# Preparing a group's pair products earlier, merging a tile later, and gathering rows three groups ahead

## The reference

```python
x = x0
for k in (k0, k1, k2):
    x = jnp.einsum('bhd,bmd,ohm->bod', x, x0, k)
    outputs.append(jnp.sum(x, axis=-1))
z = jnp.concatenate(outputs, axis=1)
h = jnp.maximum(jnp.concatenate([z, dense_ctx], axis=1) @ W_top1 + b_top1, 0.0)
h = jnp.maximum(h @ W_top2 + b_top2, 0.0)
y = h @ W_top3
```

## Time and profile before

| | us |
|---|---|
| median of 3 runs | 705.52 |
| the profiled execution | 703.25 |
| its span, first to last instruction | 701.4 |
| first chunk of stretch 0 | 42.91 |
| first chunk of stretch 15 | 615.18 |
| last chunk's end | 645.58 |

### The profile page before, as it was taken

One profiled execution on the slowest core, in us unless ns is written; L12 is line 12 of the kernel. 1 busy time (PEld: TensorE's weight loads), 2 busy tenths in 40 slices (PEclk: granted clock), 3 DMA queues, 4 the chain that ended last, 5 costly groups with the idle time before them and its releaser, 6 DMA issues.

```text
span 701.4 us, 12405 instructions
## 1 busy us (share of the span) xinstructions
PE 648.2 (92%) x2558; PEld 470.5 (67%) x2558; DVE 592.3 (84%) x1346; ACT 520.7 (74%) x1753; POOL 495.3 (71%) x443
## 2 busy tenths in 40 slices
PE   0289989899999999899999999999989999999998
PEld 0156767677676777676766767677767677777583
DVE  1649898898979898989889898989898989978890
ACT  0438877687777877777777878787777877889693
POOL 6636878687868788788878797978878884665000
PEclk9999999999999999999999999999999999999999
DMA  6362120303021211203130312121120313010100
GB/s 212 96 226 76 26 99 12 101 18 98 28 81 45 79 46 48 76 10 111 14 102 17 93 31 79 46 79 46 34 90 11 104 22 100 14 50 0 31 0 1
DMA packets 56674, 43.04 MB, mean 61 GB/s; under 512 B 37007, under 2 KB 40335, under 8 KB 56352
## 3 DMA queue, kind: packets, MB, share of 16 engines
q1 hardware_dynamic: 51488, 41.08, 19.3%
q0 software_dynamic: 5120, 1.32, 1.9%
HBM read 40.41 MB, written 1.97 MB: 60 GB/s over the span
## 4 chain that ended last, share of the span: by engine, by line
PE 45%; issue 14%; POOL 13%; DVE 13%; DMA 9%; SPq 4%; ACT 1%; DVEq 1%; POOLq 0%; ACTq 0%
PE Y L621 10%; PE Y L623 10%; PE Y L622 10%; DVE parts L535 7%; POOL x0g L320 6%; POOL parts L361 6%; PE X L588 5%; DVE pairs L475 4%; DMA pairs<-scratch 4%; SPq L275 3%; PE GB L595 2%; DMA scratch<-x0g 2%; DMA x0g<-in_table,rows_now 2%; PE X L653 1%; PE X L651 1%
## 5 line engine op out<-in xcount | busy, mean ns | idle before, releaser
L430 ACT ACTIVATE scaled<-Y,xtok 128x128 f32<-128x128 f32 x1280 | 353.4, 396 | 62.6 <-PE Y L623 60.0
L621 PE MATMUL Y<-k1lo,x1hi 128*128 128x512 f32 x640 | 294.6, 460 | 16.9 <-DVE parts L535 15.4
L623 PE MATMUL Y<-k1hi,x1lo 128*128 128x512 f32 x640 | 253.2, 396 | 0.0
L622 PE MATMUL Y<-k1hi,x1hi 128*128 128x512 f32 x640 | 252.4, 394 | 0.0
L535 DVE SCALAR_TENSOR_TENSOR parts<-Y,xtok,parts 128x128 f32<-128x128 f32 x768 | 213.1, 340 | 18.0 <-PE Y L623 17.4
L361 POOL TENSOR_TENSOR parts<-parts,scaled 128x512 f32<-128x512 f32 x128 | 185.8, 1452 | 30.2 <-ACT scaled L430 19.2
L320 POOL DMA_INDIRECT x0g<-in_table,rows_now x160 | 170.5, 1066 | 42.2 <-issue 37.5
L621 PEld LDWEIGHTS Y<-k1lo,x1hi 128*128 128x128 f32 x640 | 120.2, 188 | 74.9 <-DVE parts L535 31.9
L622 PEld LDWEIGHTS Y<-k1hi,x1hi 128*128 128x128 f32 x640 | 120.6, 188 | 40.7 <-issue 14.4
L623 PEld LDWEIGHTS Y<-k1hi,x1lo 128*128 128x128 f32 x640 | 120.2, 188 | 29.1
L475 DVE TENSOR_TENSOR pairs<-pairs,A 120x512 f32<-120x512 f32 x112 | 120.9, 1080 | 21.5 <-DMA pairs<-scratch 21.4
(11 more groups left out here) (74 smaller groups left out, 391.1 us busy)
## 6 DMA issues: line engine op xcount, KB each, us to landing
pairs<-scratch SPq DMA_DIRECT2D x112, 240.0 KB
A<-scratch SPq DMA_DIRECT2D x16, 240.0 KB
k1raw<-in_k SPq DMA_DIRECT2D x1, 2560.0 KB, 11.5
x0g<-in_table,rows_now POOLq DMA_INDIRECT x160, 2.4
k2s<-in_k SPq DMA_DIRECT2D x1, 2560.0 KB, 9.1
scratch<-x0g SPq DMA_DIRECT2D x96, 20.0 KB, 1.7
pairs<-in_w SPq DMA_DIRECT2D x3, 256.0 KB, 2.9
w2s<-in_w SPq DMA_DIRECT2D x1, 512.0 KB, 3.9
```

Of the source, the lines that this page charges most:

```text
L430: ins = nc.scalar.activation(block_of(to, i), Y[(NCH * tile + c) % YB][:, i * O:(i + 1) * O], ACT.Copy, scale=xtok[slot % 2][:, j, m:m + 1])
L621: nc.tensor.matmul(y, hi[:, tok], k1lo[:, cols], start=True, stop=False)
L622: nc.tensor.matmul(y, hi[:, tok], k1hi[:, cols], start=False, stop=False)
L623: nc.tensor.matmul(y, lo[:, tok], k1hi[:, cols], start=False, stop=True).then_inc(s_y, 1)
```

## The change

The places come from a table instead of a formula: products move to places 0, 2, 12, 20, 22, 29, 30, and the first-layer products to 12, 14, 22, 24, 26, 32, 34. A tile's merge stands behind chunk 5 of the next tile instead of chunk 2, `make_G` behind chunk 9 instead of 8. GpSimd gathers three groups ahead, 3, 2, 3 and 2 gathers in the four tiles. With two buffers for gathered rows, a gather then waits for the stores of the group that is one ahead (`s_scratch`), where it waited for products. The third group's rows are gathered before the loop.

```diff
-XTOK_AT, PROD_AT, PROD_APART, L0_LAG = 14, 6, 3.6, 6
...
-GATHER_TILES = 3
-MERGE_AT = 2
-G_AT = 8
...
+STEPS = {
+    "prod0": 0, "ph0": 1, "prod1": 2, "ph1": 4, "pl0": 9, "pl1": 10, "prod2": 12, "l0_0": 12, "l0_1": 14,
...
+    "prod5": 29, "prod6": 30, "l0_5": 32, "l0_6": 34, "x1hi": 35, "x1lo": 36, "z0": 38}
+AHEAD = 3
+MERGE_AT = 5
+G_AT = 9
...
+            pool.wait_ge(s_scratch, 16 * (FQ + AGAIN))
+            take_rows(2, 0)
+            gather(0, range(GF))
+
             def body(u, last):
                 for tile in range(GPB * TPG):
                     slot, j = tile // TPG, tile % TPG
                     T = u * (GPB * TPG) + tile
-                    gathers = not last or slot < GPB - 2
+                    g = u * GPB + slot
+                    gathers = not last or slot < GPB - AHEAD
                     if gathers and j == 0:
 
-                        pool.wait_ge(s_prod, NC0 * (u * GPB + slot + 1))
-                        take_rows(u * GPB + slot + 2, slot % 2)
+                        pool.wait_ge(s_scratch, 16 * (FQ + AGAIN) * (g + 2))
+                        take_rows(g + AHEAD, (slot + 1) % 2)
...
-                    if gathers and j < GATHER_TILES:
-                        gather(slot % 2, range(-(-GF * j // GATHER_TILES), -(-GF * (j + 1) // GATHER_TILES)))
+                    if gathers:
+                        gather((slot + 1) % 2, range(-(-GF * j // TPG), -(-GF * (j + 1) // TPG)))
```

More of the change, by code:

```diff
@@ L63 @@
 H1, H2 = 512, 256
-XTOK_AT, PROD_AT, PROD_APART, L0_LAG = 14, 6, 3.6, 6
-SPLIT_LAG = {"ph": 1, "pl": 2}
-X1_LAG = {"x1hi": 1, "x1lo": 2, "z0": 3}
-GATHER_TILES = 3
-MERGE_AT = 2
-G_AT = 8
[L76 to L85, removed]
-def prep_steps():
[L90 to L94, removed]
+STEPS = {
[3 rows of a table added]
+AHEAD = 3
+MERGE_AT = 5
+G_AT = 9
+def prep_steps():
+    return list(STEPS)
 def rank(c):
@@ L246, in steps_at @@
         def steps_at(slot, last, p):
-            return [] if last and slot == GPB - 1 else [n for n in prep_steps() if position(n) == p]
+            return [] if last and slot == GPB - 1 else [n for n in prep_steps() if STEPS[n] == p]
         @block.sync
```

## The result

The changed kernel takes 697.46 us (median of four runs, 696.67 to 698.48) and the kernel before, beside it, 705.16. The ratio of the two, estimated from all runs, is 0.9885 (95% interval 0.985 to 0.9919; the medians alone give 0.989). So it is about 1.1% faster. The forecast was 693, the range 686 to 707. The direction was right; 7.7 us were gained, where 12.5 were expected.

A forecast was written before the change was run, and what follows sets the result against it. TensorE was taken as the bound, 36.1 us a stretch without waits, with some 31 us of waits within reach. 43.4 + 2 x 38.6 + 12 x 36.6 = 559.8 against 572.27, 12.5 less, gave 693 us, range 686 to 707.

The forecast's parts named there:

- `pl0`'s price: First difference on VectorE in a steady stretch: costs TensorE 0 to 0.65 us by meeting a fold, taken as 0.4.
- the start: First group's preparation ahead of the loop: changes only in order, costing nothing, give or take 0.5 us.
- Part 1: Gathering three ahead: first roll lands 6.5 us ahead of product 0, so rolls delay nothing from stretch 1 on.
- Part 2: Steady stretch walked on VectorE and TensorE: 36.1 + 0.1 (`make_G`) + 0.4 (`pl0`) = 36.6 us.
- Part 3: Stretch 0: late roll holds product 0 and both chunks behind it; `make_G` waits 7.3, 43.4 us for 39.14.
- Part 4: Stretches 4 and 8, behind the loop's branch: `make_G` waits 2.1, so 38.6 us for 39.18 in stretch 4.
- The waits move to the first tile: Rival: products 0 and 1 wait for GpSimd's work; stretches of 37.1 to 37.55, 700 to 706 us; chance 0.26.
- VectorE enters later: Rival: VectorE enters each stretch later than 1.9 us, delaying `make_G`; at 3.6, 717 us; chance 0.10.
- No prefetch: Rival: SP still sends rolls late, every product 0 blocks as in stretch 0; well over 720 us; chance 0.04.
- Full gain: Rival: no `pl0` meets a fold, no `make_G` waits; steady stretches 36.1, 19 us less, 686; chance 0.12.

The follow-up runs named there:

- gathers_only: The new gathers (three groups ahead) with the old places, merge and `make_G`; 689.00 us, 0.9795 of the kernel before.
- places_only: The new places, merge and `make_G` with the old gathers (two groups ahead, first three tiles); 756.17 us, 1.0761 of the kernel before.
- k2s_late: The changed kernel with the load of `k2s` issued behind the loop's last roll; 688.52 us, 0.9791 of the kernel before.
- both_unrolled: The changed kernel with `k2s` loaded behind the loop, `l0_0` at place 13 and the loop over groups written out; 677.44 us, 0.9592 of the kernel before.
- l0_later: The changed kernel with the first first-layer product (`l0_0`) behind chunk 13 instead of 12; 689.84 us, 0.9806 of the kernel before.
- pl0_early: The changed kernel with the first difference (`pl0`) behind chunk 7 instead of 9; 689.87 us, 0.9774 of the kernel before.
- hold_gathers: The changed kernel with the third group's gathers held until the second group's stores have landed; 698.65 us, 0.9895 of the kernel before.
- both: The changed kernel with `k2s` issued behind the loop and `l0_0` behind chunk 13 instead of 12; 680.35 us, 0.9639 of the kernel before.

## Why the prediction was right, and what it mis-sized

The mechanism was right in each part but for TensorE's clock, whose fall it left out; `pl0`'s price, stretch 0 and the start were sized too small. In the profiled execution the change takes 698.48 against the 690.8 forecast for it, 7.7 too much: start 1.6, stretch 0 2.7, steady stretches 3.4, stretches 4 and 8 -0.1, the end 0.2. (The medians show less, as the profiled execution of before lies 1.9 below its median and that of after 1.0 above.)

- **Part 1, rolls in time: right.** The first roll goes out some 10 us ahead of the stretch that uses it (11.5 by the forecast), and from stretch 1 on no product waits for one. (The row of stores that the forecast read begins with the second of the six; the first went out at 80.32, 0.4 us earlier, which its margin covers.) gathers_only and places_only together show that this is the whole gain.
- **Part 2, the walk: right to 0.1 us** for product 0 (1.9; 2.0 measured), the merge (5.2; 5.3) and `pl0` (9.0; 9.0), and `make_G` doesn't wait. **The term that failed is `pl0`'s price**: "I take 0.4, nearer the fold's row", and TensorE's wait is 0.7 in all 12 stretches (in stretch 13 split between `make_G` and `l0_0`). The mean of 815 ns, on which the choice leaned, was a mean over differences that met a fold and others that met none. The walk had put this one into a fold, and then only the fold's row was evidence. The trace of the kernel before had settled it: in stretches 0 to 14 all 17 differences that began within a fold ended 0.55 us behind that fold's end, those near its end after 0.75 us, the others after 1.40 to 1.43; the other 28, 25 of them 0.67 or 0.68 long, had hidden this in the mean. That is most of the 12 x 0.28 = 3.4 us. The rule of the Trainium skill that was weighed there (SBUF — State Buffer, "Who interferes with whom") would have given a total of 696, nearer to the result than mine; the row of 1.42 us agrees with it.
- **Part 3, stretch 0: the right chain up to the merge, too short behind it.** 43.4 was forecast (3.5 to 5.5 lost), 46.1 measured. Product 0 starts 10.15 us into the stretch instead of 9.3 (0.85), and the merge ends as much later, at 15.2. The other 1.85 is the clock: at 0.5 TensorE's chunks 6 to 9 take 1.28 us and more instead of 0.70, and `make_G`, which was to wait for the merge, starts at 17.2. That the clock would fall when TensorE stands idle was not in the forecast. k2s_late shows that all of it hangs on the one load.
- **Part 4, stretches 4 and 8: right**, 38.53 for 38.6, with `make_G` starting 9.2 us in, behind the merge (9.1 by the forecast); both_unrolled shows that it is the branch.
- **The start: priced at nothing "give or take 0.5", it took 1.6 in this execution.** 0.85 of it is the halved clock again, which had set in ahead of the loop: two first-layer products there took 1.97 us, 1.12 to 1.13 at full clock. But l0_later and pl0_early, with the same instructions up to there, come to the first chunk at 41.45 and 43.17, so a start of 1.6 us is no more than executions differ by.
- **The rivals.** *The waits move to the first tile* didn't come: products 0 and 1 took 0.68, and all 63 products of the loop that met only gathers 0.67 to 0.69. *VectorE enters later* didn't either: 2.0 instead of 1.9. *No prefetch* is out by places_only, which shows what it would have been: 756. *Full gain* needed 36.1 a stretch, and l0_later and pl0_early show that one place in a table stood between the change's steady stretch and that.

Open stays why `k2s` and the stores behind it take as long as they do: `k2s` lands 9.1 us after its issue in the kernel before, 11.7 in the change. The gathers that run beside it were the suspect, but without them it took 11.3 (hold_gathers) and 9.4 (places_only, the same transfers up to there), and with them 9.6 in gathers_only. So single executions with the same transfers differ by 1.9 of the 2.6 us that were to be explained.

## What to carry to other kernels

Work that is moved to the head of an in-order queue takes everything behind it along when its data are late. So price the one stretch in which they are late, above all the first, where a start-up load shares the queue. When a walk puts an instruction beside one that it can collide with, take the price from the rows of such collisions and not from the mean of its group; and when only that wait is left, moving its consumer by one place may be all that is needed. Split a change into its parts: here one half made the gain, and the other half gave about half of it back until two lines were moved.

## What the runs showed of the hardware that I had not expected

**In the changed kernel TensorE's clock fell to its lower level, 1.2 GHz, after stretches in which it was partly idle.** Windows of it, cut where the granted clock changes:

```profile
35.80:41.20 5.40, 2.44 (x6) 0.78 (x6) 1.86 (x3) 0.00 (x0) 4.18 (x5) 1.00 0.92 280
41.20:48.00 6.80, 5.30 (x10) 3.06 (x11) 1.29 (x2) 1.75 (x5) 2.46 (x3) 0.50 0.81 260
48.00:54.80 6.80, 2.53 (x11) 1.69 (x9) 0.16 (x1) 0.00 (x0) 0.94 (x2) 1.00 0.33 111
54.80:61.60 6.80, 5.17 (x12) 4.16 (x13) 5.90 (x15) 6.15 (x22) 2.95 (x3) 0.50 0.20 72
```

It was busy 2.44 of 5.40 us with first-layer products that waited for VectorE, and 2.53 of 6.80 while product 0 waited. Behind each the clock is 0.5, although TensorE then had chunks to do. The waits of TensorE in stretch 0 thus cost more than their length. In `both`, with the first of these idle times about as it is here (busy 2.48 of 5.40 us, from 37.4 on), the clock stayed at 1.0, so it doesn't fall each time, and in both_unrolled it fell at 623.4 behind 6.8 us in which the profile shows TensorE busy throughout: when it falls is open; in places_only, where TensorE waits in every stretch, its mean is 0.961.

**A loop's branch cost 1.6 us on VectorE** (2.65 less 1.03), 1.53 of it shown as "issue", and with it 1.7 to 2.1 us of a stretch (38.53 for 36.88 in the change, 38.16 and 38.31 for 36.26 without it). The Trainium skill (Runtime: NRT & Kernel Launch, "Instruction fetch mechanics") says that a taken branch out of the loaded pages makes the engine fetch code first; the idle time agrees, but no run here shows that it is a fetch.

**Products over gathers stayed at 0.68 us, differences over folds did not**: held instructions ended 0.55 us behind the fold, before as after. Beside a gather it is GpSimd that was held: in stretches 0 to 14 of the changed kernel 49 gathers began within a product or a difference, and 37 of them took 1.19 to 1.50 us; the 81 others took 0.94 to 0.99. `x1lo`, which reads one operand from PSUM, was 0.68 or 0.69 over folds, before and after.
